# Embedding tower on one core: GpSimd's table look-ups issued in runs instead of one by one

## What is computed

```python
e = jnp.stack([tbl_0[ids[:, 0]], ..., tbl_31[ids[:, 31]]], axis=1)
p = e[:, ROW]; q = e[:, COL]                       # 496 pairs
kp = jnp.einsum('bpj,ipj->bpi', p, kernel)
z = jnp.sum(kp * q, axis=-1)
h = jnp.concatenate([z, dense_ctx], axis=1)
h = jnp.maximum(h @ W_top1 + b_top1, 0.0)
h = jnp.maximum(h @ W_top2 + b_top2, 0.0)
y = h @ W_top3
```

## Time and profile before

| | |
|---|---|
| median of 3 runs | 495.96 us (495.7 to 498.19) |
| profiled execution, first to last instruction | 412.5 us |
| TensorE busy | 403.7 us (98%) |
| VectorE busy | 298.6 us (72%) |
| ScalarE busy | 259.1 us (63%) |
| GpSimd busy | 231.6 us (56%) |
| TensorE clock, granted | 0.996 of full |

### The profile page before, as it was taken

How to read it: one execution, slowest core, us unless ns; L and a number is a source line. 1 busy time by engine, 2 the same in 40 slices (tenths; PEclk the granted TensorE clock), 3 DMA queues, 4 the chain that set the end, 5 groups by cost and what they waited for, 6 DMA issues and landing times.

```text
span 412.5 us, 10180 instructions
## 1 busy us (share of the span) xinstructions
PE 403.7 (98%) x3421; PEld 254.4 (62%) x3421; DVE 298.6 (72%) x293; ACT 259.1 (63%) x1874; POOL 231.6 (56%) x251
## 2 busy tenths in 40 slices
PE   7889999999999999999999999999999999999997
PEld 5556656667675766666766665666666566654442
DVE  6776887878788887878979798878879888740000
ACT  6476877667577876764796867719978667002221
POOL 6777777777677757776766777677767200000000
PEclk9998999999999999999999999999999999999999
DMA  6665661131281111211211113111311020000000
GB/s 177 210 200 155 191 221 33 27 77 27 37 219 28 29 19 47 61 28 25 63 42 28 25 25 79 24 27 26 79 25 27 15 51 2 2 2 0 2 0 1
DMA packets 18266, 24.31 MB, mean 59 GB/s; under 512 B 6387, under 2 KB 11767, under 8 KB 17958
## 3 DMA queue, kind: packets, MB, share of 16 engines
q1 hardware_dynamic: 10406, 15.64, 13.0%
q0 software_dynamic: 7808, 8.01, 9.7%
HBM read 19.44 MB, written 0.00 MB: 47 GB/s over the span
## 4 chain that ended last, share of the span: by engine, by line
PE 92%; DMA 3%; POOL 3%; issue 1%; ACT 0%
PE u_ps L690 41%; PE z_ps L724 14%; PE u_ps L711 13%; PE z_ps L730 7%; PE u_ps L771 7%; PE t_ps L644 4%; PE u_ps L791 3%; POOL nat L419 3%; DMA nat<-tbl,ids_sb 2%; PE u_ps L697 2%; DMA ids_sb<-ids 1%; PE t_ps L677 0%; PE u_ps L799 0%; ACT y_sb L571 0%
## 5 line engine op out<-in xcount | busy, mean ns | idle before, releaser
L419 POOL DMA_INDIRECT nat<-tbl,ids_sb x244 | 230.5, 945 | 90.7 <-issue 56.6
L607 DVE TENSOR_TENSOR prod<-u_ps,rows 128x1024 f32<-128x1024 f32 x184 | 213.5, 1218 | 56.7 <-PE u_ps L690 56.7
L504 ACT ACTIVATE pass_prod<-pass_prod 128x64 f32<-128x64 f32 x896 | 214.3, 243 | 22.1 <-DVE pass_prod L618 22.1
L690 PE MATMUL u_ps<-rows,k_sb 64*128 64x256 f32 x1472 | 176.2, 387 | 0.0
L504 ACT ACTIVATION_READ_ACCUMULATOR pass_prod<-pass_prod 128x1 f32 x896 | 169.9, 190 | 0.0
L690 PEld LDWEIGHTS u_ps<-rows,k_sb 64*128 64x128 f32 x1472 | 139.0, 188 | 46.0 <-DVE pass_prod L618 13.4
L618 DVE TENSOR_TENSOR pass_prod<-u_ps,nat 128x1024 f32<-128x1024 f32 x56 | 67.2, 1215 | 1.2 <-PE u_ps L711 1.2
L711 PE MATMUL u_ps<-k_sb,rows 64*128 64x256 f32 x448 | 61.5, 394 | 0.6 <-ACT rows L492 0.6
L724 PE MATMUL z_ps<-prod,sel 128*32 128x512 f32 x512 | 61.6, 598 | 0.0
L492 ACT ACTIVATE rows<-t_ps 128x512 f32<-128x512 f32 (+1 forms) x38 | 19.6, 516 | 54.2 <-PE t_ps L644 54.0
L711 PEld LDWEIGHTS u_ps<-k_sb,rows 64*128 64x128 f32 x448 | 40.6, 186 | 14.6 <-DVE prod L607 9.6
(11 more groups left out here) (50 smaller groups left out, 78.9 us busy)
## 6 DMA issues: line engine op xcount, KB each, us to landing
by_self<-rows SPq DMA_DIRECT2D x32, 128.0 KB
nat<-tbl,ids_sb POOLq DMA_INDIRECT x244
k_sb<-kern SPq DMA_DIRECT2D x3, 768.0 KB, 5.6
k_sb<-kern SPq DMA_DIRECT2D x2, 640.0 KB, 5.7
k_sb<-kern SPq DMA_DIRECT2D x1, 1152.0 KB, 5.2
k_sb<-kern SPq DMA_DIRECT2D x2, 512.0 KB
rows<-w SPq DMA_DIRECT2D x1, 1024.0 KB, 6.6
rows<-tbl SPq DMA_DIRECT2D x4, 224.0 KB
```

What stands on the lines that cost most here:

```text
L419: pool.indirect_dma_start(nat_of(m, n)[:, h * EMBED:(h + 1) * EMBED], None, tables[f], bass.IndirectOffsetOnAxis(ids_sb[:, col:col + 1], 0 ...
L504: op = nc.scalar.activation(of, of, ACT.Copy, accum_out=z_nat[:, b % 2, s, row:row + 1])
L607: nc.vector.tensor_tensor(to, u, by.unsqueeze(1).to_broadcast([P, 2, 2, SIZE]), ALU.mult).then_inc(prod_ready, 1)
L690: op = nc.tensor.matmul(u[:, h, :], k_sb[part, k_of(d), side, :], rows[part, tile, cols_of(b)], start=True, stop=True)
```

## The change

From m = 12 on, `in_front` no longer returns the last mark at or before `due`, but the nearest of a short list, `starts`. For each burst with quads the list has two marks: one when all pieces up to the one before the burst's last are done (`n - 1` pieces, with the quads of earlier bursts), and one when the burst's last piece and its quads are done (`n + 1` pieces). The look-ups of the first 12 tiles keep their marks.

```diff
@@ -128,6 +128,7 @@
 AHEAD = 30
+IN_RUNS = 12
@@ -159,6 +160,7 @@
         while self.open:
             self.add_sums(SUMS, 0)
+        self.starts = self.run_starts()
@@ -237,7 +239,22 @@
         due = first + (last - first) / (4 * (LOOKED_UP - TILES)) * (4 * (m - TILES) - AHEAD + part)
-        return max(mark for mark in self.marks if mark[0] <= max(0, due))
+        if m < IN_RUNS:
+            return max(mark for mark in self.marks if mark[0] <= max(0, due))
+        return min(self.starts, key=lambda mark: abs(mark[0] - due))
+
+    def run_starts(self):
+
+        time_of = {}
+        for now, pieces, quads in self.marks:
+            time_of.setdefault((pieces, quads), now)
+        ends = [n for n, (_, d, _) in enumerate(self.order) if len(self.quads[n])]
+        starts, quads = [], 0
+        for n in ends:
+            starts.append((time_of[n - 1, quads], n - 1, quads))
+            quads = self.quads[n][-1] + 1
+            starts.append((time_of[n + 1, quads], n + 1, quads))
+        return starts
```

## The result

The changed kernel took 508.25 us (median of 4 runs, 505.28 to 512.28) against 496.27 us of the kernel before (495.7 to 498.19). The ratio is 1.0246, with a 95% interval of 1.0187 to 1.0305: slower by some 2.5%, above the range of the forecast, whose upper end was 498.0 us.

A forecast was written before the change was run, and what follows sets the result against it. TensorE's full queue of matmuls was taken to bound the kernel, with look-ups hidden behind it. The profiled 412.5 us + 0 + 0 + 0 stayed 412.5 us, so the measured median stayed: 496.0 us, range 495.2 to 498.0.

The forecast's parts named there:

- What bounds the kernel: From 45 to 322 us TensorE is always busy, 38.00 of 38.00 us a stretch; look-ups cost only if landing late.
- Part 1, the rate: GpSimd issues look-ups every 1.25 us in a run, as already before, with 15.2 us spare; cost 0.
- Rival 2: Slower: issues inside a run cost more and GpSimd becomes the bound, 500.5 us at 0.15 us extra; 3 in 100.
- Part 2, the landings: Rows land 2.1 us after issue, typically 1.5 us later than before, yet ahead of their transposes; cost 0.
- The pair: Tiles 58 and 59, the tightest case: slack before TensorE's transposes falls from 2.4 to 0.3 to 0.8 us.
- The pair 24 and 25: Next tightest tiles, beside busy DMA engines: the row lands by 124.6 us at worst, transposes start at 124.75.
- The sum: Profiled 412.5 us plus three zeros; measured median 495.96 us, its extra 83.5 us taken as untouched: 496.0 us, no change.
- Rival 1: Faster: look-ups slow TensorE's passes by 0.1 us and runs remove it, saving 4.7 us, 491.3 us; 5 in 100.
- Rival 3: Slower: a GpSimd halt of 2.84 us just ahead of tile 59 exceeds the slack, 497.7 to 498.2 us; 8 in 100.
- Rival 4: GpSimd lags its gates so look-ups keep nearly the same rhythm; 496.0 us, within the forecast; 24 in 100.

The follow-up runs named there:

- plain_dma: Kernel before with look-ups of tiles 12 to 63 replaced by plain transfers of the same size at the same gates: 431.53 us, ratio 0.8791.
- before_again: The kernel before, unchanged, run again for its trace in a disturbed (slow) series: 496.27 us, ratio 0.9998.

## Why the prediction was wrong

- **What bounds the kernel.** Right for the trace it was read from, and for calm series: there TensorE is full from 45 to 322 us, but for the one wait of 1.2 us, and the changed kernel is within 0.5% of the kernel before. Wrong for the timed runs, where TensorE idles 32.6 of 337.2 us in the kernel before.
- **Part 1, the rate.** Right in both conditions: 0.94 us an issue, 1.25 us from one to the next in a run. Rival 2 did not happen.
- **Part 2, the landings.** The pair was right and one term was too small. I took 0.3 to 0.8 us to be left; in a calm series TensorE waited 1.16 us. GpSimd took up the gate after 0.81 us, as far as I had allowed, but TensorE started 303.94 - 300.32 = 3.6 us after the last issue, and I had counted 2.1 us, to the end of the packets only. The last of the sixteen steps of the counter took 3.5 us. The pair 24 and 25 did not wait.
- **The sum.** This is the step that failed. "I know nothing in the change that touches that part" was said of 83.5 us that I took to lie around the program. They lie inside it: the changed kernel's span is 507.4 of 509.14 us. And the change does touch them: it cost 12 us (508.25 against 496.27) where they are and 1.3 us (414.03 against 412.71) where they are not. I added a change computed for one condition to a median of another. The gap, a sixth of the time, should have been named as the largest unknown of the sum, with a wide range for it.
- **Rival 1** had the right subject, look-ups that disturb the other engines, and the wrong sign for the runs. I gave it 5 in 100 on the strength of matmuls and multiplications that are equally fast with and without look-ups. That comparison was sound for its trace, and could not show what does not happen in it.
- **Rival 3** priced one halt of GpSimd. In the disturbed traces such halts are common, and not of GpSimd alone: VectorE, TensorE and ScalarE stand as well.
- **Rival 4** holds in part in a calm series. Look-ups there stand in rows of up to 31 in the kernel before and up to 38 in the changed one. In a disturbed one the rows are short (6 and 7 at most) and the gates count: a mean of 3.1 before and 4.2 after.

Why runs cost more than single look-ups is shown only in part. That the indexed look-ups hold back wake-ups, and that kernels with long rows cost more than the kernel before, the runs show. That the changed kernel loses its 1.8 to 2.5% by longer rows and not by their places is likely, by the late wake-ups of each row, and not shown. Part of the loss is TensorE's lower clock, which comes and goes: 30.7 us of it in one trace and 17.1 us in the other. Why a series is calm or disturbed is open. One more difference was seen: the nine calm traces hold 5,884 to 5,965 changes of semaphores each, and the nine disturbed ones of kernels that issue all their look-ups by index from 2,430 to 3,077; `plain_dma`, in a disturbed series, holds 5,385. Most of what is missing are the steps of landings. Whether the recording and the holding have a common cause was not tried.

## What to carry to other kernels

Before a sum is made on a trace, hold its span against the timed runs: if a sixth of the time is not in it, the trace may be of another condition, as here, and a range drawn from it does not hold for the timed one. An instruction on an engine that never sets the end can still cost everyone, by delaying the news that others wait for; compare a waiting engine's start with the end of what it waits for, and not only the lengths of instructions. To find out what a background transfer costs, replace it by a plain one of the same size before changing its schedule.

## What was not expected of the hardware

In disturbed series an indexed look-up from GpSimd (128 rows of 256 bytes, 0.95 us of GpSimd) cost the program 0.27 us each beside a nearly full TensorE, and a plain transfer of the same size (0.54 us of GpSimd) nothing that shows: 273.00 of 273.00 us busy. While a run of look-ups goes on, counters change late, and engines that wait on them start late, by up to 5.0 us in the changed kernel and up to 21.3 us without gates. Most of this time ends 0.9 to 1.6 us after the last issue of a run is over (53.7 of 73.4 us in `before_again`, 54.7 of 81.8 us in the changed kernel, the first 0.05 us of each counted in). The same program on the same inputs takes 413 us in one series and 495 us in another.
